# Semaphore clears moved into the experts' block, two query loads moved one block later, GpSimd's first all-reduce and the order of the feed-forward part changed, in a two-layer Perceiver kernel

## What is computed

```python
x = x + _L0_xattn_ref(ctx_1024, _layernorm(x), mask, ...)      # 16 heads of 16
x = x + _L0_attn_ref(_layernorm(x), ...)                       # causal, spectral-normed weights
x = x + _L0_ffn_ref(_layernorm(x), ...)                        # 12 experts, 3 routed
x = x + _L1_xattn_ref(_layernorm(x), ctx_1024, ctx_1024, ...)  # 16 heads of 64
x = x + _L1_attn_ref(_layernorm(x), ...)
x = x + _L1_ffn_ref(_layernorm(x), w_gate, w_up, w_down)
```

```python
x = act_qdq(x)
up = act_qdq(x @ lpbq_dequant(w_up).T)
gate = act_qdq(x @ lpbq_dequant(w_gate).T)
sig = fixed_qdq_u16(sigmoid(gate))
gate = act_qdq(gate * sig)
o = act_qdq(gate * up)
return o @ lpbq_dequant(w_down).T
```

## Time and profile before

| | us |
|---|---|
| median of 3 runs | 1743.44 (1739.8 to 1745.81) |
| the profiled execution: its time | 1739.34 |
| its span in the profile | 1737.6 |
| busy: PE, DVE, ACT, POOL | 1554.7, 1120.5, 888.9, 687.4 |
| mean granted clock of TensorE | 0.953 |

### The profile page before, as it was taken

The page is one execution under the profiler, slowest core; times in us unless marked ns, Lnnn a source line. Parts: engine busy times, 40 slices in busy tenths (PEclk is TensorE's granted clock), DMA queues, the critical chain, the costliest instruction groups (busy, mean ns, idle before and its releaser), DMA issues. The chain is left out here.

```text
span 1737.6 us, 42209 instructions
## 1 busy us (share of the span) xinstructions
PE 1554.7 (89%) x15980; PEld 876.2 (50%) x15980; DVE 1120.5 (64%) x1789; ACT 888.9 (51%) x1204; POOL 687.4 (40%) x536
## 2 busy tenths in 40 slices
PE   3999999999499999999787957999999999986774
PEld 1454455455223333333353424777777777773442
DVE  3656656656399999999236737666666666604536
ACT  2555555555257777777351113555555555541535
POOL 1431000000111111111061306999999999960710
PEclk8999999999779999999899988999999999997897
DMA  4697987978632222221210037565565555212000
GB/s 163 177 216 225 217 249 207 233 231 195 170 105 67 66 66 66 66 66 50 100 57 1 1 95 233 137 157 157 143 160 145 141 145 157 78 35 92 2 1 13
DMA packets 178077, 212.14 MB, mean 122 GB/s; under 512 B 57080, under 2 KB 151428, under 8 KB 173342
## 3 DMA queue, kind: packets, MB, share of 16 engines
q1 hardware_dynamic: 177376, 210.37, 45.1%
q10 hardware_dynamic: 576, 0.00, 0.0%
HBM read 122.71 MB, written 87.57 MB: 121 GB/s over the span
## 5 line engine op out<-in xcount | busy, mean ns | idle before, releaser
L1130 POOL TENSOR_TENSOR x_r<-x_p 128x1024 f16<-128x1024 f32 x256 | 479.3, 1895 | 23.9 <-ACT x_p L1106 17.1
L1145 DVE TENSOR_REDUCE x_mx<-a_all 128x2 f32<-128x1024 f32 x249 | 304.9, 1225 | 147.8 <-PE a_all L1029 147.8
L1106 ACT ACTIVATE x_p<-s_all 128x1024 f32<-128x1024 f32 x256 | 248.4, 1022 | 223.2 <-PE s_all L1012 223.2
L711 ACT ACTIVATE x_p<-s_all 128x1024 f32<-128x1024 f32 x256 | 261.2, 1024 | 48.7 <-PE s_all L621 41.3
L766 DVE TENSOR_REDUCE x_mx<-a_all 128x1 f32<-128x512 f32 x352 | 229.7, 682 | 15.9 <-PE o_all L632 8.8
L1012 PE MATMUL s_all<-x_q,x_k 64*128 64x256 f16 x3072 | 209.5, 269 | 0.0
L1047 PEld LDWEIGHTS o_all<-x_v,x_p 128*128 128x128 bf16 x2048 | 178.8, 97 | 40.7 <-issue 40.7
L1047 PE MATMUL o_all<-x_v,x_p 128*128 128x129 f16 x2048 | 197.4, 221 | 0.9 <-POOL x_r L1130 0.9
L1048 PE MATMUL o_all<-x_v,x_r 128*128 128x65 f16 x2048 | 192.6, 193 | 0.4 <-issue 0.4
L1048 PEld LDWEIGHTS o_all<-x_v,x_r 128*128 128x128 f16 x2048 | 180.7, 98 | 0.0
L1012 PEld LDWEIGHTS s_all<-x_q,x_k 64*128 64x128 f16 x3072 | 149.2, 94 | 62.0 <-issue 0.8
(11 more groups left out here) (356 smaller groups left out, 2779.4 us busy)
## 6 DMA issues: line engine op xcount, KB each, us to landing
values<-vst SPq DMA_DIRECT2D x16, 2064.0 KB, 10.5
x_v<-values SPq DMA_DIRECT2D x32, 1032.0 KB, 5.3
keys<-kst SPq DMA_DIRECT2D x32, 1024.0 KB, 7.0
x_k<-keys SPq DMA_DIRECT2D x128, 256.0 KB, 5.2
x_k<-keys SPq DMA_DIRECT2D x192, 64.0 KB, 2.1
values<-vst SPq DMA_DIRECT2D x16, 528.0 KB, 12.7
x_v<-values SPq DMA_DIRECT2D x32, 264.0 KB, 2.6
cf<-in_ctxT SPq DMA_DIRECT2D x16, 512.0 KB, 9.6
```

The lines of the kernel that those rows point to most:

```text
L711: act.activation(prob[g % NP][:], chip.s_ps[g % 2][:].rearrange("p (c q) -> p c q", q=SQ), ACT.Exp, scale=hd ** -0.5).then_inc(p_ready, 1)
L1106: act.activation(prob[g % NP][:], chip.s_ps[g % 2][:].rearrange("p (c q) -> p c q", q=SQ), ACT.Exp, scale=hd ** -0.5).then_inc(p_ready, 1)
L1130: pool.tensor_tensor(rest[g % NP][:], prob[g % NP][:], hi, ALU.subtract).then_inc(rest_done, 1)
L1145: dve.tensor_reduce(mx[a[1] % 2][:, n // 4, 2 * (n % 4):2 * (n % 4) + 2], chunk_banks(u, g)[:, :].rearrange("p (h c) -> p h c", h=2), AX.X ...
```

## The change

- `recycle_semaphores` goes. At the start of the experts the semaphores used so far are taken out of use (`retire_semaphores`), and SyncE clears them inside the experts' block; the experts get new ones. The three semaphores of the experts' weights, which are still in use, are made in the outer scope (`lasting_sem`) and aren't cleared.
- The query loads of units 2 and 3 move from the end of the projection's block into the cross-attention's block, behind the keys of unit 2 and ahead of the wait for the first turn.
- The all-reduce over a constant leaves layer norm 5. One over a column of scales, into a tile that nobody reads, stands at the end of GpSimd's work in self-attention s1.
- In the feed-forward part ScalarE rounds two gate tiles ahead of the first sigmoid and the other four one by one between the sigmoids, where before all six came first. VectorE's order follows: `gate_back` of tiles 3 to 5 comes between silu products, and the up maxima too; the last up maximum and `largest` of up come with and behind the fourth silu. Three `up_back` instead of four come ahead of scale 3.

```diff
--- before.py
+++ after.py
@@ -67,30 +67,15 @@
         self.sems.append(self.sem_scope.enter_context(self.nc.semaphore(name)))
         return self.sems[-1]
 
-    def recycle_semaphores(self):
-
-        sems, self.sems = self.sems, []
-        with self.nc.Block() as block:
...
-        self.sem_scope.close()
+    def lasting_sem(self, name):
+
+        return self.ctx.enter_context(self.nc.semaphore(name))
+
+    def retire_semaphores(self):
+
+        old = self.sems, self.sem_scope
+        self.sems, self.sem_scope = [], self.ctx.enter_context(ExitStack())
+        return old
 
 
 def load_constants(chip, x_dram, query_weight, context):
@@ -156,7 +141,6 @@
                 pool.wait_ge(var, 1)
                 pool.tensor_tensor(rs[:], ve[:], chip.half[:, 0:NT], ALU.pow).then_inc(rstd, 1)
                 if scales is not None:
-                    pool.partition_all_reduce(scales.idle[:], chip.half[:, 0:1], P, bass.bass_isa.ReduceOp.absmax)
                     scales.over_rows(pool, 0)
 
             @block.tensor
@@ -858,8 +842,6 @@
                 for u in range(2):
                     buffers.load_queries(sp, 0, u)
                 buffers.load_keys(sp, 0, 1)
-                for u in range(2, 4):
-                    buffers.load_queries(sp, 0, u)
 
             @block.tensor
             def _(pe):
@@ -963,6 +945,8 @@
 
                 buffers.load_values(sp, 0, 0)
                 buffers.load_keys(sp, 0, 2)
+                for u in range(2, 4):
+                    buffers.load_queries(sp, 0, u)
                 sp.wait_ge(qm_turned, 32)
                 buffers.load_values(sp, 0, 1)
                 buffers.load_keys(sp, 0, 3)
@@ -1694,12 +1678,12 @@
         self.uw = chip.sb("ew_uw", [DA, 3 * L], F32, scope)
         self.bb = chip.sb("ew_bb", [L, D], F32, scope)
         self.router = ((self.pw[:], pT.rearrange("(k p) n -> p k n", p=P)), (self.uw[:], uT), (self.bb[:], b2))
-        self.router_loaded = chip.sem("ew_rld")
+        self.router_loaded = chip.lasting_sem("ew_rld")
         self.src = (w1T, w2T)
         self.ws = [chip.sb(f"ew{i}", [P, KT, 12 * D], F32, scope) for i in range(2)]
         self.hi = [chip.sb(f"ewh{i}", [P, KT, 12 * D], F16, scope) for i in range(2)]
         self.lo = [chip.sb(f"ewl{i}", [P, KT, 12 * D], F16, scope) for i in range(2)]
-        self.loaded, self.split = chip.sem("ew_ld"), chip.sem("ew_split")
+        self.loaded, self.split = chip.lasting_sem("ew_ld"), chip.lasting_sem("ew_split")
 
     def loads(self, sp):
         for i in range(2):
@@ -1737,6 +1721,7 @@
     L, DA = 12, 64
     R = 3
     NC3 = R * NT
+    old_sems, old_scope = chip.retire_semaphores()
     with ExitStack() as scope:
         pw, uw, bb, ld = weights.pw, weights.uw, weights.bb, weights.router_loaded
         xh = [chip.sb(f"{tag}_xh{i}", [P, KT, TOK], F16, scope) for i in range(2)]
@@ -1762,6 +1747,11 @@
             return slice(0, NT) if layer == 0 else slice(NT, NC3)
 
         with nc.Block() as block:
+            @block.sync
+            def _(sp):
+                for s in old_sems:
+                    sp.sem_clear(s)
+
             @block.gpsimd
             def _(pool):
                 pool.wait_ge(compared, 2 * L)
@@ -1952,6 +1942,7 @@
                     if n < 2:
                         hidden_low(2 + n)
                 dve.wait_ge(acc, 4 * NTL)
+    old_scope.close()
 
 
 MAGIC = 12582912.0
@@ -1968,6 +1959,7 @@
         self.w = [chip.sb(f"{tag}_w{i}", [P, self.NBK, 32], F32, scope) for i in range(3)]
         self.s = [chip.sb(f"{tag}_s{i}", [P, self.NBK], F32, scope) for i in range(3)]
         self.r = [chip.sb(f"{tag}_r{i}", [P, self.NBK], F32, scope) for i in range(3)]
+        self.largest = chip.sb(f"{tag}_largest", [P, 1], F32, scope)
         self.chip = chip
         self.loaded, self.step, self.scaled, self.tr, self.kept = (chip.sem(f"{tag}_{n}") for n in ("ld", "step", "scaled", "tr", "kept"))
         self.jobs = []
@@ -2031,6 +2023,7 @@
             link(pool.tensor_scalar(w[:], w[:], MAGIC, MAGIC, ALU.add, ALU.subtract))
             link(pool.tensor_scalar(w[:], w[:], 7.0, -8.0, ALU.min, ALU.max))
             link(pool.tensor_tensor(w[:], w[:], wide(s), ALU.mult))
+        link(pool.partition_all_reduce(self.largest[:], self.s[0][:, 0:1], P, bass.bass_isa.ReduceOp.absmax))
 
 
 class FeedForwardScales:
@@ -2038,7 +2031,6 @@
 
     def __init__(self, chip, tag, scope):
         self.am, self.ar, self.sc, self.rc = (chip.sb(f"{tag}_{n}", [P, 5], F32, scope) for n in ("am", "ar", "sc", "rc"))
-        self.idle = chip.sb(f"{tag}_idle", [P, 1], F32, scope)
         self.found, self.spread = chip.sem(f"{tag}_amd"), chip.sem(f"{tag}_ard")
 
     def over_rows(self, pool, i):
@@ -2143,20 +2135,21 @@
                 largest(1, 0, I6)
                 scale(1)
                 dve.sem_inc(scale_done, 1)
-                for m in range(I6):
-                    gate_back(m)
-                    if m in (1, 3, 5):
-                        up_max(m // 2)
-                silu_max(0)
-                up_max(3)
-                silu_chunk(0)
-                for m in range(1, 4):
+                gate_back(0)
+                up_max(0)
+                gate_back(1)
+                gate_back(2)
+                up_max(1)
+                for m in range(4):
                     silu_max(m)
                     if m < 3:
-                        up_max(3 + m)
-                    silu_chunk(m)
-                    if m == 2:
-                        largest(2, 1, 2 * I6 + 3)
+                        gate_back(3 + m)
+                        silu_chunk(m)
+                        up_max(2 + m)
+                    else:
+                        up_max(2 + m)
+                        silu_chunk(m)
+                        largest(2, 1, 2 * I6 + 4)
                 scale(2)
                 dve.sem_inc(scale_done, 1)
                 for m in range(4, I6):
@@ -2164,12 +2157,12 @@
                     silu_max(m)
                     silu_chunk(m)
                 largest(3, 2, 3 * I6)
-                for m in range(4):
+                for m in range(3):
                     up_back(m)
                 scale(3, 2.0 ** -16 / QM)
                 link(dve.tensor_scalar(rc[:, 3:4], rc[:, 3:4], 2.0 ** -16, None, ALU.mult))
                 dve.sem_inc(scale_done, 1)
-                for m in range(4, I6):
+                for m in range(3, I6):
                     up_back(m)
                 product(0)
                 for m in range(1, I6):
@@ -2239,9 +2232,11 @@
                 act.wait_ge(magic_set, 2)
                 act.activation(warm[:], magic[:, 0:1], ACT.Sigmoid)
                 act.wait_ge(scale_done, 1)
-                for m in range(I6):
+                for m in range(2):
                     rounded(gate[:, m, :], gate_bank[m], 1, gate_round)
                 for m in range(I6):
+                    if m < 4:
+                        rounded(gate[:, m + 2, :], gate_bank[m + 2], 1, gate_round)
                     sigmoid(m)
                     sigmoid_round(m)
                     if m < 4:
@@ -2315,7 +2310,6 @@
 
                 layer_norm(chip, "ln2")
                 experts(chip, "moe", expert_weights)
-        chip.recycle_semaphores()
 
 
         with ExitStack() as scope:
```

## The result

| | before | after |
|---|---|---|
| median, same chip | 1741.47 (1738.47 to 1748.35) | 1746.43 (1742.19 to 1751.32) |
| profiled execution: time, span | 1739.34, 1737.6 | 1748.41, 1746.5 |
| mean granted clock of TensorE | 0.953 | 0.945 |

After takes 1.0029 times as long, 95% interval 1.0019 to 1.0039: 5.0 us more (3.3 to 6.8), a small loss that is clear of the noise. The forecast was 1745.2 us, in a range of 1738 to 1750.5, from a sum of +1.75 us. The direction held and the time fell into the range, but the difference was larger than the sum.

What follows compares the result with a forecast made beforehand. Each block waits for its slowest engine, so edits count where they change which ends last. Terms -4.5 - 4.3 + 3.6 + 4.5 + 1.25 + 1.2 = +1.75 us on 1743.44 gave 1745.2 us, range 1738 to 1750.5.

Steps and rivals of the forecast that it cites:

- Semaphores: Before layer norm 3: a block and its barrier go, SyncE's clears stay hidden; 4.5 us gained, bounds 4.3 and 5.0.
- Queries: End of the query projection: VectorE ends the block instead of SyncE's loads; 4.3 us gained, bounds 4.1 and 4.3.
- Sum in self-attention: End of self-attention: GpSimd's all-reduce with its code load now ends the block, 3.6 us later, bounds 3.5 and 4.8.
- the quiet row: Layer norm 5 before the change: the all-reduce waited 5.94 us of "issue" away from DMA, taken as its load price.
- Layer norm 5: Power starts 4.8 us later, its load running from the block's start; block ends 4.5 us later, bounds +4.0 and +6.6.
- Rival 1: Layer norm 5: the code load is paid at the call, behind the wait; +9.2 instead of +4.5, 1749.9 us, chance 0.14.
- the way back: Layer norm 5: GpSimd's code load for a TENSOR_TENSOR behind an all-reduce, 6.9 to 7.8 us in the rows, 6.9 taken.
- Rival 2: Layer norm 5: the power runs with the all-reduce's code in place; 3.3 us earlier than now, 1737.4 us, chance 0.10.
- TensorE's clock: Projection after self-attention: 4.7 us idle may leave it partly at half clock; 0 to 5 us lost, 1.2 taken.
- rival 3: Projection after self-attention: all of it at half clock; +5 instead of +1.2, 1749.0 us, chance 0.08.
- Feed-forward: Feed-forward part: last up maximum and largest fall behind the fourth silu, second scale 1.25 us later, bounds 1.1 and 1.6.
- Sum and base: Whole kernel: terms sum to +1.75 us; the median of three runs, 1743.44 us, is the base, giving 1745.2 us.

Runs made afterwards that it cites:

- four dummies: The changed kernel with four dummy 128x512 TensorE matmuls behind the last turned output of self-attention s1: ratio to before 1.0012, 1747.42 us.
- root_scalar: The changed kernel with layer norm 5's root taken by ScalarE and its reciprocal by VectorE: ratio to before 0.9966, 1737.49 us.
- all_but_pool: The changed kernel without the all-reduce in self-attention, the idle one kept in layer norm 5: ratio to before 0.9957, 1737.67 us.

## Why the prediction was right, and where it was off

- **Semaphores, -4.5.** Measured -4.48. The clears of SyncE took 7.4 us, below the 10 estimated, all hidden.
- **Queries, -4.3.** The gap went as said (0.36 us idle left). The stage gained 3.5. The step left out that the projection q1's own matmuls run in part at half clock, and that how much of them varies: the stage took 29.86, 30.15 and 28.04 us in three kernels with the old loads, and 26.2 to 26.4 or 24.9 to 26.0 in those with the new. That is a gain of 3.1 to 3.9 between like executions. The slack said to be 5.4 us was 4.7.
- **Sum in self-attention, +3.6.** In after +2.2, since the attention and GpSimd's work before the sum were both over some 1.4 us earlier in this execution; with four dummies, where they weren't, +3.4. The load was 5.81 us; the 5.94 taken from the quiet row was the right price.
- **Layer norm 5, +4.5.** Measured +5.2, and 14.9 to 15.4 us in the five kernels that have it against 10.1 to 10.25: +4.95 on average. The mechanism held: the load starts with the block and runs beside the wait. Rival 1, the load paid behind the wait, would have put the power 6.9 us behind 1668.08; it stood 5.6 behind. That alone would leave room for a load of 5.6 us paid behind the wait; what speaks against it is the all-reduce of the same block, whose load did run beside its wait, and the price of the way back with no wait, below. Rival 2 fell with the late power. The mis-sized term is the way back, 7.2 to 7.6 us in the five kernels where the low end, 6.9, was taken. The argument for the low end was that all rows of that kind lie among DMA and this place is quiet. The trace of before had a dearer pair, from the first chain of this kind, which I did not read:

```profile
61.56 0.40 POOL L1354 PARTITION_ALL_REDUCE sq_q<-sq_q  x1 [5.81 <-issue]
...
69.58 3.00 POOL L1357 TENSOR_TENSOR sq_wu<-sq_w,sq_a 128x768 f32<-128x768 f32 x2 [7.62 <-issue]
```

  It has 5.81 us there and 7.62 back among DMA, as after has 5.81 and 7.64 in the quiet: quiet made neither way cheaper. A rule of the Trainium skill priced the load at about 6 us ("GPSIMD Engine Reference", section 2.1); by the traces the way to the all-reduce agrees (5.81 to 5.94), and the way back doesn't where nothing is waited for (7.62).
- **TensorE's clock, +1.2: the step that failed.** It measured +3.8 in after and 3.6 to 3.8 in two more kernels with the wait. I had both ends (0 and 5) and chose from where 4.7 us of idleness lay between two falls, 2.5 and 5.4 us behind the last matmul. Here it fell 3.1 us behind, 1.6 us ahead of the projection, and nearly all of that ran slow. On this term rival 3 is what happened: it had a chance of 0.08, and its price (+5) was nearer the truth. What the earlier trace rows could have told is that a wait of 4.7 us lies past one of two observed falls, so "the clock is gone before the work starts" deserved an even chance. In the four kernels with the unfilled wait the fall came 3.1 to 3.4 us behind the last matmul; what varied more is the return. With root_scalar, whose TensorE waited 4.58 us, it came 6.8 us behind the fall and the projection took 8.83; in after it came 10.2 us behind.
- **Feed-forward, +1.25.** Measured +1.24 to the second scale and +1.12 to the fourth. The stage differs by 2.75 us between the two profiled executions, since the down matmuls stayed at half clock longer (13.5 us from first start to last end, in place of 12.2). That is scatter: the stage took 59.9 to 60.7 us in five executions with the old order (mean 60.3) and 60.9 to 62.7 in six with the new (mean 61.6), +1.4.
- **Sum and base.** With the means, -4.5 - 3.5 + 5.5 (from layer norm 4 to 5: 87.1 in four kernels with the old place of the sum, 92.6 in four with the new and TensorE not filled) + 4.95 + 1.4 = +3.85 us, against a measured 5.0 (3.3 to 6.8). The forecast came nearer to the time than to the difference, and that is luck: the three runs it stood on had a median 2 us above that of twenty, and the sum was 3.2 us short, so the two errors took off each other. By the prediction's own line of 0.3% for what can be told from no change, after counts as the same by 0.01%; with twenty runs a side the difference is nevertheless clear of zero.

What stays open: in all_but_pool, the kernel without GpSimd's early sum, TensorE waited only 1.1 us ahead of the projection, and yet the clock was at half from 1658.5 to 1661.5, inside it, and the projection took 8.25 us. The other kernels with so short a wait took 6.56 to 6.85. So a wait is not the only thing after which the clock falls, and no run tells what brought that fall about.

## What to carry to other kernels

A code load of GpSimd is only moved, not saved, as long as another kind of operation stands between two of the same kind: count the changes of kind in the new order, and give each its load, from the start of the block in which the next operation stands. Put one where the engine has nothing to do and the block is long enough, or take the odd operation off the engine. A wait that is put ahead of TensorE has a second price, the clock of all that follows; dummy matmuls just long enough to end with the wait give it back, and where a part has long pauses between matmuls anyway they can shorten it, here by 4.3 to 4.6 us, where the order of its operations was worth 1.4.

## What the runs showed of the hardware that was not expected

- The way back from the all-reduce's code to a power took 7.2 to 7.6 us from the block's start in a quiet stretch (five kernels), more than the way there (5.8 to 6.0). In after it overlapped a wait that ended 2.02 us into it.
- ScalarE changes its tables for less than GpSimd its code: the table load ahead of the root took 1.28 us, and VectorE waited 1.06 us in all for it, where it waited 6.70 us for the power in after.
- A dummy matmul of 128x512 in f32 leaves two records, each of 0.59 us, that start some 0.44 us apart; nine took 7.89 us.
- Twenty-five dummy matmuls and one more at its start kept the granted clock at 1.00 through the feed-forward part, where the same kernel without them had 0.77 on average.
